# Weighing of value tiles moved to GpSimd and VectorE in the last thirteen steps, and turns on TensorE moved between its lifts

## The reference

```python
Q = (einsum('nc,rch->rnh', x, Wq) + bq).reshape(R, N, HEADS, OUT)      # K and V alike
q_i, k_j, v_j = Q[edge_type, dst], K[edge_type, src], V[edge_type, src]
score = sum(q_i * k_j, axis=-1) * scale
seg = dst * R + edge_type
e = exp(score - segment_max(score, seg)[seg])
alpha = e / segment_sum(e, seg)[seg]
out = segment_sum(v_j * alpha[..., None], dst).reshape(N, HD) + bias
return layernorm(x + out)
```

## Time and profile before

| | us |
|---|---|
| median of 3 runs | 2265.75 |
| lowest, highest | 2263.09, 2269.71 |
| the profiled execution | 2287.36 |
| its span | 2285.5 |

### The profile page before, as it was taken

One profiled execution on the slowest core, in us unless ns is written; L12 is line 12 of the kernel. 1 busy time (PEld: TensorE's weight loads), 2 busy tenths in 40 slices (PEclk: granted clock), 3 DMA queues, 4 the chain that ended last, 5 costly groups with the idle time before them and its releaser, 6 DMA issues.

```text
span 2285.5 us, 33477 instructions
## 1 busy us (share of the span) xinstructions
PE 1686.4 (74%) x7580; PEld 1156.2 (51%) x7597; DVE 1566.4 (69%) x3882; ACT 1056.2 (46%) x4084; POOL 1180.8 (52%) x1261
## 2 busy tenths in 40 slices
PE   8999994227999994476667676667776667676778
PEld 4555541003444442355556555556665556565667
DVE  8888983002433442587878888878888878888877
ACT  3333320001000000057767776767776767777775
POOL 3111127763666204656666666666666666666514
PEclk9999997658999996699999999999999999999998
DMA  8988737765999737888888888888888888888733
GB/s 231 276 237 232 211 117 240 226 195 200 320 332 331 253 151 235 259 274 262 285 277 275 276 284 276 277 284 276 274 277 282 278 280 281 266 280 275 247 114 113
DMA packets 346899, 574.72 MB, mean 251 GB/s; under 512 B 45265, under 2 KB 239985, under 8 KB 346702
## 3 DMA queue, kind: packets, MB, share of 16 engines
q0 software_dynamic: 87920, 276.07, 39.9%
q1 hardware_dynamic: 225770, 235.79, 31.4%
q10 hardware_dynamic: 33012, 60.73, 7.2%
HBM read 411.99 MB, written 140.96 MB: 242 GB/s over the span
## 4 chain that ended last, share of the span: by engine, by line
PE 31%; POOL 26%; issue 23%; DVE 11%; another core or an unknown queue 6%; ACT 2%; DMA 1%; SPq 0%; DVEq 0%; ACTq 0%; POOLq 0%
POOL region L543 26%; PE sums L715 20%; PE sums L784 4%; PE pairs L795 3%; DVE region L1110 3%; DVE region L1311 1%; PE sums L842 1%; PE sums L853 1%; ACT region L982 1%; DVE region L1234 1%; DVE region L1235 1%; DVE region L1236 0%; ACT acc L1000 0%; DVE region L1368 0%
## 5 line engine op out<-in xcount | busy, mean ns | idle before, releaser
L543 POOL DMA_INDIRECT region<-kv_tab,kvidx x831 | 811.3, 976 | 582.6 <-issue 196.6
L715 PE MATMUL sums<-region,acc 128*128 128x512 f32 (+2 forms) x1568 | 676.5, 583 | 7.5 <-ACT acc L867 4.9
L982 ACT ACTIVATE region<-region 128x64 f32<-128x64 f32 x2392 | 662.2, 346 | 0.9
L795 PE MATMUL pairs<-region 128*128 128x256 f32 x1664 | 433.3, 405 | 204.9 <-DVE region L1311 115.9
L784 PE MATMUL sums<-region 128*128 128x131 f32 x3328 | 459.2, 293 | 150.6 <-issue 144.5
L784 PEld LDWEIGHTS sums<-region 128*128 128x128 f32 x3328 | 427.7, 203 | 209.1 <-issue 196.3
L715 PEld LDWEIGHTS sums<-region,acc 128*128 128x128 f32 (+1 forms) x1568 | 297.0, 194 | 308.3 <-issue 284.7
L795 PEld LDWEIGHTS pairs<-region 128*128 128x128 f32 x1664 | 316.5, 200 | 268.2 <-issue 227.3
L1279 DVE TENSOR_TENSOR region<-sums,region 128x512 f32<-128x512 f32 (+1 forms) x215 | 146.4, 690 | 373.7 <-PE sums L715 163.2
L525 POOL DMA_INDIRECT region<-q_tab,region x288 | 273.6, 950 | 156.1 <-issue 81.8
L1000 ACT COPY acc<-sums 128x256 f32 x832 | 303.7, 365 | 96.6 <-remote 51.6
(11 more groups left out here) (244 smaller groups left out, 969.3 us busy)
## 6 DMA issues: line engine op xcount, KB each, us to landing
region<-q_seg SPq DMA_DIRECT2D x832, 128.0 KB
kv_tab<-region ACTq DMA_DIRECT2D x42, 1280.0 KB
q_seg<-region SPq DMA_DIRECT2D x288, 128.0 KB
q_tab<-region SPq DMA_DIRECT2D x48, 640.0 KB, 4.2
region<-rel_tab SPq DMA_DIRECT2D x208, 128.0 KB
region<-region POOLq DMA_DIRECT2D x47, 384.0 KB, 5.5
region<-kv_tab,kvidx POOLq DMA_INDIRECT x831
region<-in_x SPq DMA_DIRECT2D x96, 128.0 KB, 3.1
```

The lines of the kernel that those rows point to most:

```text
L543: pool.indirect_dma_start(ring_row[:, a:a + 2 * C], None, kv_tab, bass.IndirectOffsetOnAxis(ap=kvidx[:, t:t + 1], axis=0)).then_inc(s_got[ ...
L715: done = nc.tensor.matmul(bank[o % 4][0:n, 0:w], acc[:, k, t * P:t * P + n], w_sb[:, k, :, :].rearrange("p u c -> p (u c)")[:, c0:c0 + w], ...
L795: done = nc.tensor.matmul(qk[:, i, :], oht[:, s % 2, i * P:(i + 1) * P], qring[:, s % QS, i, :], start=True, stop=True)
L982: done = nc.scalar.activation(ring_v[:, i, spot(q), h * D:(h + 1) * D], ring_v[:, i, spot(q), h * D:(h + 1) * D], ACT.Copy, scale=alT[:, h ...
```

## The change

In the steps that drain, GpSimd weighs tiles 0 and 1 (one TENSOR_TENSOR of 128x256 each, under a new semaphore `s_pay_pool`), VectorE tiles 2 and 3, ScalarE none. On TensorE `weights_a(s)` moves from behind the lift of s + 1 to its middle, between the second and third tile, and the turn of the quotient (k = 5) moves from `weights_b` to `weights_a`, so ahead of the sums; where there is no lift any more, `weights_a(s)` stands ahead of the sums. On ScalarE `weights_a` of odd k comes behind the rest of the weighing. The copy to `alT` waits for GpSimd too, and so does GpSimd's memset.

```diff
+    POOLT = 2
...
         def act_tiles(q):
-            return SB - 1 if q < DRAIN else 1
+            return SB - 1 if q < DRAIN else 0
+
+        def pool_tiles(q):
+            return 0 if q < DRAIN else POOLT
...
-            return (SB - 1) * min(q, DRAIN) + max(q - DRAIN, 0)
+            return (SB - 1) * min(q, DRAIN)
...
+            for q in range(DRAIN, NSB):
+                pool.wait_ge(s_alT, q // PERC + 1)
+                pool.wait_ge(s_got[q % KL], gathered(q))
+                for i in range(pool_tiles(q)):
+                    v = ring_v[:, i, spot(q), :].rearrange("p (h d) -> p h d", h=H)
+                    g = SB * (q % PERC) + i
+                    nc.gpsimd.tensor_tensor(v, v, alT[:, :, g:g + 1].broadcast_to([P, H, D]), ALU.mult
+                                            ).then_inc(s_pay_pool, 1)
             pool.wait_ge(s_lift, NSB)
             pool.wait_ge(s_mul, NSB)
+            pool.wait_ge(s_pay_pool, POOLT * (NSB - DRAIN))
...
                 if k == 3:
                     turn_rows(c, 1)
+                if k == 5:
+                    pe.wait_ge(s_al, c + 1)
+                    nc.tensor.transpose(bank[6][:, P:2 * P], al[:], ident[:]).then_inc(s_aT, 1)
...
                 if k == 3:
                     turn_carries(c, 1)
-                if k == 5:
-                    pe.wait_ge(s_al, c + 1)
-                    nc.tensor.transpose(bank[6][:, P:2 * P], al[:], ident[:]).then_inc(s_aT, 1)
...
                     if i < act_tiles(q):
                         pe.wait_ge(s_pay, paid(q) + i + 1)
+                    elif i < pool_tiles(q):
+                        pe.wait_ge(s_pay_pool, POOLT * (q - DRAIN) + i + 1)
...
                 for i in range(SB):
+                    if i == SB // 2:
+                        weights_a(s - 1)
                     done = nc.tensor.matmul(qk[:, i, :], oht[:, s % 2, i * P:(i + 1) * P], qring[:, s % QS, i, :],
...
                 if s + 1 < NSB:
                     lift(s + 1)
-                weights_a(s)
+                else:
+                    weights_a(s)
...
                         act.wait_ge(s_pay_dve, PERC * c)
+                        if PERC * c > DRAIN:
+                            act.wait_ge(s_pay_pool, POOLT * (PERC * c - DRAIN))
...
-                if s < NSB:
+                if s < NSB and piece(s)[1] % 2 == 0:
                     weights_a(s)
                 for i, pair in pieces[3:]:
                     payload(u, i, pair)
+                if s < NSB and piece(s)[1] % 2 == 1:
+                    weights_a(s)
...
-                tiles = range(act_tiles(u), SB) if 0 <= u < NSB else []
+                tiles = range(act_tiles(u) + pool_tiles(u), SB) if 0 <= u < NSB else []
```

More of the change, by code:

```diff
@@ L334, in gnn_kernel @@
         s_pay_dve, s_placed, s_cols = sem("s_pay_dve"), sem("s_placed"), sem("s_cols")
+        s_pay_pool = sem("s_pay_pool")
         s_r1, s_r2, s_r3, s_r4, s_r5, s_r6, s_r7, s_r8, s_r9 = (sem(f"s_rec_{n}") for n in (
@@ L1371, in payload @@
             def payload(q, i):
-                if i == act_tiles(q):
+                if i == act_tiles(q) + pool_tiles(q):
                     dve.wait_ge(s_alT, q // PERC + 1)
```

## The result

Over 20 executions of each the change takes 2275.23 us in the median (2269.14 to 2282.51), the kernel before 2266.18 (2256.32 to 2272.75): ratio 1.0036, interval 1.0026 to 1.0046. Slower by 9 us, where 5.7 us faster was forecast, and just outside the range. The profiled execution of the change took 2277.28 us, 2275.5 of them span.

A forecast was written before the change was run, and what follows sets the result against it. It took an outside pace of 6.163 us a step to bound the main loop and ScalarE to set the drain. Gains of 4.4 + 2.2 less 0.9, 5.7 us off the 2265.75 median, gave 2260.1, range 2256 to 2264.

The forecast's parts named there:

- VectorE beside GpSimd: After the last gather, GpSimd's weighings slow VectorE: 0.9 us lost on the path, 3.5 us in the drain hidden.
- The slack of 4.5 us: In the drain, VectorE's step stays 0.56 us below ScalarE's 2.30, over eight steps, hiding the collisions.
- port held for a whole instruction: Rival, drain: each of 26 GpSimd weighings stops VectorE for half its length, 11.0 us lost, 2270; chance 0.15.
- ScalarE weighs no tile: Drain: four activations fewer a step bring ScalarE from 2.83 to 2.30 us a step, 4.4 us gained.
- the drain does not shorten: Rival, drain: sums, not ScalarE, set it, or the turn only moves the wait; 2265, no change; chance 0.06.
- The quotient's turn: End of the last chunk: TensorE turns the last weights ahead of the sums, 2.2 us gained, bounds 0 to 3.1.
- GpSimd's weighing: Drain: 1.19 us for each of 26 tiles, the last sixteen ending at 2215.5, just hidden.
- The main loop: Before the last gather: if the outside pace holds, the moved turns and copies cost and gain nothing.
- lifts held up by the turn: Rival, main loop: turns amid lifts delay sums, 0.9 us in about 18 of 25 chunks, 16 us, 2276; chance 0.10.
- my bound for a pace that holds: Main loop sign: forecast wrong if the gather groups' pace moves by more than 0.02 us a step, 3.4 in all.

The follow-up runs named there:

- e5_psum: The change, but in the steps that drain VectorE's one-hots read the column numbers from PSUM, not SBUF; 2272.93 us, ratio 1.0027.
- e2_pool: The kernel before with GpSimd's weighings alone (two tiles GpSimd, two VectorE), all turns in their old places; 2291.83 us, ratio 1.0022.
- e11_one: The kernel before's main loop, early quotient turn; in the drain GpSimd one tile behind the one-hots, VectorE three, ScalarE none; 2266.96 us, ratio 0.9996.
- e1_orders: The kernel before with only the change's new places of the turns; ScalarE keeps one tile, GpSimd none; 2287.54 us, ratio 1.0006.
- e9_tail: The kernel before with only the end changed: early quotient turn, VectorE weighs all four tiles in the drain; ratio 0.9997 on a quick chip.
- e8_actodd: The kernel before with only ScalarE's other order in odd steps (copies behind the weighings); ratio 0.9976 on a quick chip.
- e7_again: Repeat of the kernel before with only TensorE's turns of rows placed between the products of a lift; 2272.55 us, ratio 1.0015.
- unchanged: The kernel before, as it is, run as a kernel of its own for a second profile; 2267.59 us, ratio 1.0000.
- e3_paced: The change, but GpSimd waits before each pair of weighings for VectorE's one-hots of the step before; 2290.57 us, ratio 1.0010.
- whole: The whole change again, against the kernel before, on a quick chip (kernel before 1914.18 us); ratio 1.0027.
- whole_again: The whole change once more, against the kernel before, on a quick chip (kernel before 1914.47 us); 1918.63 us, ratio 1.0026.
- e6_late: The change, but GpSimd waits for the last scores before its first weighing; 2273.86 us, ratio 1.0030.
- e10_both: The change with the kernel before's main-loop orders, GpSimd starting after the last scores, and drain one-hots reading column numbers from PSUM; 2269.93 us, ratio 1.0014.

## Why the prediction was wrong, point by point

Added up, the change's +9.05 us are: last gather to scores +7.7, scores to weights -2.8, placements +3.4, the final stage -1.0, and +1.7 in the part before, which is by subtraction.

- **VectorE beside GpSimd: the step that failed.** I priced 26 meetings at 0.44 us each from one weighing beside GpSimd's comparisons, counted a fifth of VectorE's step ahead of the last scores as exposed because only that reads two operands, put 0.9 us on the path and hid 3.5 in the drain. A one-hot has one tensor operand, and it is shut out all the same, for a whole weighing when the two alternate (0.65 us for 0.28) and for all ten when they don't (6.38 us; 5.57 for a weighing). Measured: +7.7 on the way to the scores, and in the drain, against the same kernel without GpSimd, 30.73 - 27.06 = +3.7 us up to VectorE's last reduction. That is near the 3.5 that I had worked out; the slack of 4.5 us that was to hide it wasn't there. How much it is up to the scores depends on which of the two happens: +2.1 to +4.1 in `e5_psum` and `e2_pool`, where they alternated. How often the other executions of the change stood for all ten, no trace shows.
- The rival "port held for a whole instruction" had the mechanism, at 0.15. I set it back on the word of rows with another operation. It gave 2270, since it too let the weighings pass one by one and took no account of TensorE's clock. The Trainium skill's rule ("SBUF — State Buffer", section "SBUF: two separate sides") names an exclusive lock between GpSimd and VectorE, for VectorE's instructions with two inputs in SBUF or in a two-port mode. The trace agrees, with 0.65 for 0.28 us a one-hot, and with 1.12 us for four from PSUM beside the weighings and 1.13 away from them. That a waiting instruction can be passed over ten times in a row, the measured 6.38 us, is more than the rule says.
- **ScalarE weighs no tile: -4.4.** Without GpSimd the placements end 1.3 to 1.7 us sooner (25.0 to 25.4 for 26.7), but VectorE's last reduction, which the final stage waits for, ends where it did (27.1 to 27.5 for 27.3), since VectorE with four tiles sets 2.42 us a step and its additions come late. So nothing of the 4.4 was won in any kernel here. The rival "the drain does not shorten", at 0.06, had the outcome, with VectorE and not the sums in ScalarE's place. What the change would have won with VectorE's two at no cost to it, no run here could show.
- **The quotient's turn: -2.2.** Right in mechanism, and near in size: 19.06 for 21.81 in the change, 19.19 for 22.12 in `e11_one`, where ScalarE has no tile either. With ScalarE's tile kept (`e1_orders`) it is 1.6, and 1.2 in `e9_tail` (20.94, against 22.12 in `e8_actodd`).
- **GpSimd's weighing, 1.19 us a tile.** It takes 0.61 undisturbed, at the low bound; the Trainium skill's price ("GPSIMD Engine Reference", section 3.1), an estimate of 0.6, was the better one. Being quick helped nothing: the quick ones came back to back, and there VectorE stood for 6.38 us.
- **The main loop: 0.** The rival "lifts held up by the turn" gave 16 us; 5.0 by subtraction in `e7_again`, and 1.7 in the change, where ScalarE's order (-3.3) pays part of it back. Right in sign, far too large in size. On chips of one median the last gather ends at 2145.5 in the change and at 2142.0 in `unchanged`, 0.02 us a step apart, my bound for a pace that holds. Single executions near that median end it anywhere from 2136 to 2148, so this difference decides nothing.

## What to carry to other kernels

Work given to GpSimd beside a busy VectorE is not free because GpSimd is idle: look at what VectorE executes in those microseconds, not only at its two-operand instructions (here one-hots waited too, and a reduction didn't). Price each meeting at the whole GpSimd instruction, and a series issued back to back at its whole length. If GpSimd must help, let it wait between pieces (that brought the scores' copy back from 21.5 to 13.6 us in `e3_paced`, though the drain only from 30.7 to 29.6). And set VectorE's own time for the work (0.41 us a tile here) against what the meetings cost before moving it. Before crediting an engine that comes free, find which engine the next stage waits for: here it was VectorE's last reduction, not ScalarE's last placement.

## What the hardware showed that I had not expected

- Ten GpSimd instructions of 0.6 us in a row held one VectorE instruction for 6.38 us (5.57 in `whole`, 5.59 in `whole_again`), while in four other kernels (`e2_pool`, `e5_psum`, `e6_late`, `e10_both`) VectorE got its turns between them. What decides which of the two happens is open.
- It goes both ways: GpSimd's weighing took 0.87 us instead of 0.61 beside VectorE's.
- A pause of 3.06 us on TensorE was followed, from 2198 us on, by 4 us at a granted clock of 0.50 and 4 us at 0.81, in the second of which TensorE was busy all the time with its late steps.
- The kernel before took 1914, 2266 and 2288 us on different chips. The change's last stretch, from the weights' copy on, was alike on two of them (89.5 us, and 89.8 and 90.4). An order that loses on one chip can gain on another.
